# A recurrence with a feed-forward network beside it: plain fp32 products in four 32-column strips in place of split fp32r products

## The chip, the cores and the metric

The kernel runs on one core of one Trainium2 chip. The metric is the device time of one execution in microseconds, and the figure given is the median of several executions. TensorE is shown by the trace as two engines, PE (matmuls) and PEld (weight loads); DVE is VectorE, ACT is ScalarE, POOL is GpSimd, SP issues the DMAs. One plain fp32 matmul of the program stands in the trace as two records, an fp32r matmul as one.

## The reference, cut to what matters

Four layers act on x of shape (16, 256, 256), each added to its input. The first two (attention, a gated linear recurrence) are not touched but for a side job in the first. The third is a mixture of experts with a shared network, the fourth is a recurrence over 256 steps:

```python
# third layer: out is the sum over the routed experts
shared = jax.nn.gelu(context_c @ sw1 + sb1, approximate=True) @ sw2 + sb2
return out + shared
# fourth layer
xw = jnp.einsum('ntd,dh->nth', x, Wx) + b
def step(prev_h, xw_t):
    next_h = jnp.tanh(xw_t + prev_h @ Wh)
    return (next_h, next_h)
_, hs = jax.lax.scan(step, h0, jnp.swapaxes(xw, 0, 1))
```

sw1 is 256 x 1024, sw2 is 1024 x 256, Wx and Wh are 256 x 256.

## The kernel before, in words

All data lie transposed, features on the 128 partitions. The program has three blocks: attention and linear recurrence, then the experts, then the last stage, `shared_and_rnn`, which is the subject here.

An fp32 product is made in one of two ways. Plain: one matmul on fp32 operands. Split: each operand is parted into a high half rounded to fp32r and the rest (`xhi` and `xlo`, `ghi` and `glo`, weights in two versions), and three fp32r matmuls (high by high, high by rest, rest by high) add up in PSUM. The experts use the split form. Their weights are split once, by POOL in the attention block (`split_piece`, two instructions for each of 40 pieces of 128 x 512), written to DRAM and read again.

The last stage does two things at once. The recurrence has 256 steps. In step k TensorE multiplies the state by `wh` (`recur`, L1720: 2 halves of the contraction x 4 strips; the state is the stationary operand, 128 x 32, the weights move, 64 columns, and strip j writes PSUM partitions 32j to 32j+31), DVE transposes the result out of PSUM (L1825), ACT takes tanh (L1800), and its result is the state of step k+1. In even steps TensorE also computes x times `wx` for the next two steps (`drive`, L1731, the same shape). In odd steps DVE copies the bias into the PSUM bank used next (L1828).

Between the steps TensorE works off the shared network of the third layer for 14 chunks of 16 time steps (256 columns each; the first two chunks were done in the experts' block and are kept as `y0`). A generator, `all_ffn`, yields the matmuls in a fixed order and `quota(k)` says how many follow step k: 4 to 6 in the first 16 steps, then 5.75 on average, after 12 ahead of step 0. There are 96 matmuls a chunk: 8 up products and 8 down products of 2 x 3 fp32r matmuls, all with 128 x 128 weights and 256 columns. After an up product ACT takes gelu (L1809), then DVE splits the result (`split`: cast L1833, subtraction L1835), and down products read the split parts. When a chunk is done, DVE adds its two halves to x (`add_x`, L1846), which fills `xc`, the input of `drive` 16 steps later; it waits until POOL has used the buffer's former content (`staged_done`). POOL adds state and input for every chunk of 16 steps (L1873), and SP sends the sum out.

In-order engines: DVE serves the transposes, the splits and `add_x` from one queue, ACT tanh and gelu from one, TensorE everything from one.

Of the kernel before, what the change touches and what calls it, by code (L numbers as in the profile page):

```python
# [12 lines left out]
P = 128  # L13
# [97 lines left out]
def build(nc, x_tok, x_dm, small_in, mod_w, w_qkv, w_out, w_fih, ew1, ew2, sw1, sw2, wx, wh, out):  # L111
# [13 lines left out]
    with hold:  # L125
# [7 lines left out]
        halves = nc.dram_tensor("weight_halves", (NE + 1, 2, P, 2, DC * F), fp32).ap()  # L133
# [15 lines left out]
def attention(nc, env):  # L149
# [5 lines left out]
    with st:  # L155
# [68 lines left out]
        def piece(n):  # L224

            e, w, q = n // 8, n // 4 % 2, n % 4
            if w == 0:
                src = env["ew1"][e] if e < NE else env["sw1"]
                src = src[(q // 2) * P:(q // 2 + 1) * P, (q % 2) * PIECE:(q % 2 + 1) * PIECE]
            else:  # L230
                src = env["ew2"][e] if e < NE else env["sw2"]
                src = src[2 * q * P:2 * (q + 1) * P].rearrange("(c p) d -> p c d", p=P)
            return src, env["halves"][e, w, :, :, q * PIECE:(q + 1) * PIECE]
# [20 lines left out]
        def pieces_to(r):  # L254

            return max(0, 2 * (r + 1) + min(r + 1, 10))
# [1031 lines left out]
CH = 16  # L1288
NCH = T // CH
PIECE = 512  # L1290
PIECES = 8 * (NE + 1)
# [4 lines left out]
def experts(nc, env):  # L1296
# [9 lines left out]
    with st:  # L1306
        xhi = sb(st, "xhi", [P, DC, B, T], fp32r)
        xlo = sb(st, "xlo", [P, DC, B, T], fp32r)
        w1 = sb(st, "w1", [P, 2, 2, DC, F], fp32r)
        w2 = sb(st, "w2", [P, 2, 2, FC, D], fp32r)  # L1310
# [5 lines left out]
        y0 = raw1[:, :, 0:FIRST * T]  # L1316
# [15 lines left out]
        with ExitStack() as routed:  # L1332
            g = sb(routed, "g", [P, RING, T])
# [12 lines left out]
            room = env["wfih_sb"][:].rearrange("p c n -> p (c n)")  # L1346
# [24 lines left out]
            def _(sp):  # L1371
# [9 lines left out]
                load_weights(sp, JOBS, halves[NE:NE + 1], up_done, down_done)  # L1381
# [12 lines left out]
            def _(act):  # L1394
# [241 lines left out]
def shared_and_rnn(nc, env, ex):  # L1636
# [4 lines left out]
    xhi, xlo, w1, w2, wx, wh = (ex[k] for k in ("xhi", "xlo", "w1", "w2", "wx_sb", "wh_sb"))  # L1641
    N = B * CH
    BUF = TOP * B % 2
# [4 lines left out]
    ITEMS = 6  # L1648
    AHEAD = 12
    st = ExitStack()  # L1650
    with st:  # L1651
# [3 lines left out]
        staged = ex["raw1"][:, :, 2 * N:4 * N].rearrange("p s (t c b) -> p s t c b", t=CH, c=DC)  # L1655
        row1 = sb(st, "row1", [P, 2 * B])
        g = ex["raw2"][:, 0:RING]
        ghi = sb(st, "ghis", [P, RING, N], fp32r)
        glo = sb(st, "glos", [P, RING, N], fp32r)
# [8 lines left out]
        up_ok, gelu_ok, hi_ok, lo_ok, down_ok = (sem(st, n) for n in ("up_ok", "gelu_ok", "hi_ok", "lo_ok", "down_ok"))  # L1668
# [6 lines left out]

        FFN = 2 * ITEMS * FC

        def step_of(end):

            at = -1  # L1680
            taken = AHEAD
            while taken < end:
                at += 1
                taken += quota(at)
            return at
# [7 lines left out]
        def up_step(c, f):  # L1693
            return step_of(FFN * (c - FIRST) + (ITEMS * (f + 1) if f < 3 else 2 * ITEMS * f - ITEMS))

        def down_step(c):
            return step_of(FFN * (c + 1 - FIRST))

        gelus_in, splits_in, adds_in = ({k: [] for k in range(-1, T)} for _ in range(3))
        for c in range(FIRST, NCH):  # L1700
            for f in range(FC):
                k = up_step(c, f)
                gelus_in[k].append((c, f))
                splits_in[k + 1 if k >= 0 else k].append((c, f))
            k = down_step(c)
            adds_in[k + 1 if k >= 0 else k].append(c)
# [6 lines left out]
        def _(pe):  # L1713
# [20 lines left out]
            def ffn(c, xs):  # L1734

                for n in range(FC + 2):
                    if n < FC:
                        pe.wait_ge(gelu_ok, FC * (c - FIRST) + n + 1)
                        for k in range(DC):
                            whi, wlo = (w1[:, BUF, v, k, n * P:(n + 1) * P] for v in range(2))  # L1740
                            dst = ph[n % RING][:, 0:N]
# [5 lines left out]
                            if k == DC - 1:  # L1747
                                i.then_inc(up_ok, 1)
                            yield
                    if n >= 2:  # L1750
                        f = n - 2
                        pe.wait_ge(lo_ok, FC * (c - FIRST) + f + RING + 1)
                        if f == 0 and c > FIRST:
                            pe.wait_ge(x_ready, c)
                        hi, lo = ghi[:, f % RING], glo[:, f % RING]
                        for m in range(DC):
                            whi, wlo = (w2[:, BUF, v, f, m * P:(m + 1) * P] for v in range(2))
                            dst = py[:, m, 0:N]
                            nc.tensor.matmul(dst, whi, hi, start=(f == 0), stop=False)  # L1759
                            yield  # L1760
                            nc.tensor.matmul(dst, whi, lo, start=False, stop=False)  # L1761
                            yield
                            i = nc.tensor.matmul(dst, wlo, hi, start=False, stop=(f == FC - 1))  # L1763
# [4 lines left out]
            def all_ffn():  # L1768
                for c in range(FIRST, NCH):
                    yield from ffn(c, (slice(None), slice(0, B), slice(CH * c, CH * (c + 1))))  # L1770

            pe.wait_ge(ex["wxh_in"], 32)
            for w in range(2):
                for h in range(2):
                    pe.wait_ge(ex["w_in"][w][h][BUF], 16 * (TOP * B // 2 + 1))
            work = all_ffn()
            for _ in range(AHEAD):
                next(work, None)
            pe.wait_ge(row1_set, 1)
# [6 lines left out]
            for k in range(T):  # L1786
# [3 lines left out]
                for _ in range(quota(k)):  # L1790
                    next(work, None)

        @block.scalar
        def _(act):
            def recur(k):
                q, s, at = k // CH // 2, k // CH % 2, k % CH
                act.wait_ge(pre_ready, k + 1)
                if at == 0:
# [4 lines left out]
            for k in range(-1, T):  # L1803
                if k >= 0:
                    recur(k)
                for c, f in gelus_in[k]:
                    act.wait_ge(up_ok, FC * (c - FIRST) + f + 1)
                    act.wait_ge(lo_ok, FC * (c - FIRST) + f + 1)
                    nc.scalar.activation(g[:, f % RING], ph[f % RING][:, 0:N], ACT.Gelu_apprx_tanh,  # L1809
# [3 lines left out]
        def _(dve):  # L1813
            def bias_of_state():
                dve.wait_ge(zeroed, 2)
# [21 lines left out]
            def add_x(c):  # L1837
                s = c % 2
                if c >= FIRST:
                    dve.wait_ge(down_ok, FC * (c + 1 - FIRST) + RING)  # L1840
                dve.wait_ge(staged_done[s], 2 * PRIMED + 2 * (c // 2))
                for m in range(DC):
                    y = py[:, m, 0:N].rearrange("p (b t) -> p b t", b=B)
                    if c < FIRST:
                        y = ex["y0"][:, m].rearrange("p (b t) -> p b t", b=B)[:, :, CH * c:CH * (c + 1)]
                    i = nc.vector.tensor_tensor(xc[:, s, m].rearrange("p t b -> p b t"), XT[:, m, :, CH * c:CH * (c + 1)],  # L1846
                                                y, ALU.add)
                    i.then_inc(half_added if m == 0 else x_ready, 1)

            for k in range(-1, T):  # L1850
                if k >= 0:
                    recur(k)
                for c in adds_in[k]:
                    add_x(c)
                if k < 0:
                    for c in range(FIRST):
                        add_x(c)
                    bias_of_state()
                for c, f in splits_in[k]:
                    split(c, f)  # L1860

        @block.gpsimd
        def _(pool):
            nc.gpsimd.memset(row1[:], 0.0).then_inc(zeroed, 1)  # L1864
            pool.wait_ge(zeroed, 1)
            nc.gpsimd.memset(row1[0:1, :], 1.0).then_inc(row1_set, 1)
            nc.gpsimd.memset(hs[:], 0.0).then_inc(zeroed, 1)

            def stage(q, s):
                pool.wait_ge(h_ready, CH * (2 * q + s + 1) + 1)  # L1870
                pool.wait_ge(out_done[s], 16 * PRIMED + 16 * q)
# [3 lines left out]
            with pool.Fori(0, NCH // 2) as i:  # L1875
                stage(i, 0)
                stage(i, 1)
# [67 lines left out]
```

## Time and profile before

| | us |
|---|---|
| median of 3 executions | 1309.77 (1305.39 to 1312.52) |
| the profiled execution, its own time | 1305.88 |
| span of the profiled execution | 1304.1 |
| PE busy in the span | 1216.4 (93%) |
| DVE busy | 879.0 (67%) |
| ACT busy | 623.2 (48%) |
| POOL busy | 333.9 (26%) |

The span begins with the first and ends with the last instruction of the program; the profiled execution's own time is 1.8 us longer. The profile can split a span into stretches and give each engine's busy time in them, group instructions by line and shape, or list them in order of time. A matmul's record runs from when its first column enters to a modelled end, so records overlap: the distance from one start to the next tells what a matmul costs, not its length.

### The profile page before, as it was taken

How to read it: one execution, taken by the hardware profiler on the slowest of the kernel's cores; microseconds unless marked ns; L12 is line 12 of the kernel's file. 1: busy time of each engine (PE TensorE's matmuls, PEld its weight loads, DVE VectorE, ACT ScalarE, POOL GpSimd, SP SyncE). 2: the span in 40 equal slices, each digit the busy share in tenths (PEclk: the TensorE clock that was granted, in tenths of full speed). 3: DMA queues.
4: the chain of work that ended last, by engine and by line, in shares of the span. 5: the costliest groups of instructions: out<-in, count | busy, mean ns of one | idle time of the engine just before them, and what ended most of it. 6: DMA issues, size and time to landing. Idle time of an engine off the chain costs nothing. (4 is left out here: it accounts for less than half of the span.)

```text
span 1304.1 us, 34455 instructions
## 1 busy us (share of the span) xinstructions
PE 1216.4 (93%) x14104; PEld 961.0 (74%) x14104; DVE 879.0 (67%) x2047; ACT 623.2 (48%) x1168; POOL 333.9 (26%) x311
## 2 busy tenths in 40 slices
PE   3789999999999988499999999999999999999995
PEld 2456666766665433159999999999978888888883
DVE  6788888888775889957666666666655555555552
ACT  2377777777777879433333333333323333333331
POOL 1436566465552679600000000000010000000000
PEclk9699999999999999799999999999999999999995
DMA  9013242332212100059999999999900000000000
GB/s 359 3 50 99 85 136 74 123 99 86 87 50 82 64 1 1 0 203 397 378 368 360 368 363 371 365 366 361 370 11 19 11 19 11 20 11 19 11 19 18
DMA packets 82507, 190.39 MB, mean 146 GB/s; under 512 B 4144, under 2 KB 15536, under 8 KB 82096
## 3 DMA queue, kind: packets, MB, share of 16 engines
q1 hardware_dynamic: 82352, 188.21, 40.2%
q8 instruction: 112, 1.84, 0.6%
q14 instruction: 43, 0.35, 0.1%
HBM read 162.76 MB, written 25.17 MB: 144 GB/s over the span
## 5 line engine op out<-in xcount | busy, mean ns | idle before, releaser
L1417 ACT ACTIVATE g<-ph,b 128x256 f32<-128x256 f32 x256 | 121.6, 475 | 247.9 <-PE ph L1606 247.8
L693 DVE TENSOR_REDUCE mx<-pR 128x4 f32<-128x1024 f32 x128 | 156.4, 1225 | 62.7 <-PE pR L899 61.4
L1825 DVE STREAM_TRANSPOSE preT<-pr 128x64 f32<-128x64 f32 x256 | 63.9, 250 | 157.7 <-PE pr L1720 155.7
L1800 ACT ACTIVATE hs<-preT 128x32 f32<-128x32 f32 x256 | 58.8, 230 | 217.2 <-DVE preT L1825 217.0
L1526 DVE CAST ghi<-g 128x256 fp32r<-128x256 f32 x256 | 74.8, 292 | 128.2 <-ACT g L1417 128.0
L1622 PE MATMUL py<-ghi,w 128*128 128x256 f32 x512 | 145.7, 285 | 1.7 <-DVE glo L1528 1.6
L1604 PE MATMUL ph<-xhi,w 128*128 128x256 f32 x512 | 145.3, 284 | 0.0
L1605 PE MATMUL ph<-xlo,w 128*128 128x256 f32 x512 | 144.9, 283 | 0.0
L1623 PE MATMUL py<-glo,w 128*128 128x256 f32 x512 | 144.9, 283 | 0.0
L1624 PE MATMUL py<-ghi,w 128*128 128x256 f32 x512 | 144.9, 283 | 0.0
L1606 PE MATMUL ph<-xhi,w 128*128 128x256 f32 x512 | 144.9, 283 | 0.0
L490 ACT ACTIVATE raw<-pR 128x1024 f32<-128x1024 f32 x128 | 129.2, 1024 | 17.7 <-PE pR L908 16.1
L1720 PE MATMUL pr<-wh_sb,hs 128*32 128x64 f32 x4096 | 114.0, 231 | 10.2 <-ACT hs L1800 10.2
L1528 DVE TENSOR_TENSOR glo<-g,ghi 128x256 fp32r<-128x256 f32 x256 | 108.9, 426 | 8.8
L1720 PEld LDWEIGHTS pr<-wh_sb,hs 128*32 128x32 f32 x4096 | 71.4, 112 | 47.5 <-ACT hs L1800 15.5
L1873 POOL TENSOR_TENSOR raw<-xc,hs 128x256 f32<-128x256 f32 x32 | 23.5, 756 | 323.7 <-ACT hs L1800 323.7
L1864 POOL MEMSET row<- 128x32 f32 x1 | 0.1, 125 | 404.3 <-POOLq L1332 404.3
L1622 PEld LDWEIGHTS py<-ghi,w 128*128 128x128 f32 x512 | 98.2, 192 | 3.2 <-DVE glo L1528 3.1
L1605 PEld LDWEIGHTS ph<-xlo,w 128*128 128x128 f32 x512 | 98.3, 192 | 0.2 <-issue 0.2
L1604 PEld LDWEIGHTS ph<-xhi,w 128*128 128x128 f32 x512 | 98.3, 192 | 0.2 <-issue 0.2
L1606 PEld LDWEIGHTS ph<-xhi,w 128*128 128x128 f32 x512 | 98.3, 192 | 0.0
L1623 PEld LDWEIGHTS py<-glo,w 128*128 128x128 f32 x512 | 98.2, 192 | 0.0
(226 smaller groups left out, 2898.1 us busy)
## 6 DMA issues: line engine op xcount, KB each, us to landing
w<-weight_halves SPq DMA_DIRECT2D x132, 1024.0 KB, 8.0
weight_halves<-wparts SPq DMA_DIRECT2D x40, 512.0 KB, 3.9
modw<-in_ew SPq DMA_DIRECT2D x32, 256.0 KB, 4.5
xn<-in_x_tok SPq DMA_DIRECT2D x4, 1024.0 KB, 11.8
XT<-in_x_dm SPq DMA_DIRECT2D x2, 2048.0 KB, 14.6
out_dm<-raw SPq DMA_DIRECT2D x16, 256.0 KB, 2.0
modw<-in_sw SPq DMA_DIRECT2D x8, 256.0 KB, 4.5
raw<-in_sw SPq DMA_DIRECT2D x2, 1024.0 KB, 7.7
```

Of the source, the lines that this page charges most:

```text
L490: nc.scalar.activation(probs[:, j % 4], pR[k][:], ACT.Exp, scale=HD ** -0.5).then_inc(free[k], 1)
L693: nc.vector.reduce_max(mx[:, :, 2 * j:2 * j + 2].rearrange("p t s -> p s t"), pR[k][:].rearrange("p s (t k) -> p s t k", t=TC), AX.X).then ...
L1417: nc.scalar.activation(g[:, t % RING], ph[t % RING][:, 0:T], ACT.Gelu_apprx_tanh, bias=b1[:, n, f:f + 1]).then_inc(gelu_done, 1)
L1526: nc.vector.tensor_copy(ghi[:, t % RING], g[:, t % RING]).then_inc(hi_done, 1)
L1528: nc.vector.tensor_tensor(glo[:, t % RING], g[:, t % RING], ghi[:, t % RING].bitcast(fp32), ALU.subtract).then_inc(lo_done, 1)
L1604: nc.tensor.matmul(dst, whi, hi, start=(k == 0), stop=False)
L1605: nc.tensor.matmul(dst, whi, lo, start=False, stop=False)
L1606: i = nc.tensor.matmul(dst, wlo, hi, start=False, stop=(k == DC - 1))
L1622: nc.tensor.matmul(dst, whi, hi, start=(f == 0), stop=False)
L1623: nc.tensor.matmul(dst, whi, lo, start=False, stop=False)
L1624: i = nc.tensor.matmul(dst, wlo, hi, start=False, stop=(f == FC - 1))
L1720: i = nc.tensor.matmul(dst[QW * j:QW * (j + 1)], prev[:, c], quad(wh[:, c], j), start=False, stop=(c == DC - 1), skip_group_check=True)
```

## The change

The shared network of the last stage is computed in plain fp32. Its weights are taken from `raw1` and `raw2`, fp32 copies that are in SBUF since the end of the attention block; the split versions of the shared weights are no longer made (`PIECES` falls from 40 to 32), stored or read (`load_weights` of job `JOBS` is gone). Each product is issued as four matmuls with 128 x 32 weights (`strips`), the form that `recur` and `drive` have. Up products are made in two halves of 128 columns, an item each; down products stay at 256 columns. `quota(k)` now counts in halves: an up item counts 1 and a down item 2, 4 for each step, and 3 in every fourth step from step 64; nothing is issued ahead of step 0. The input x of the network is put together again by POOL as `xf = xhi + xlo` (`whole_x`, 128 x 512, one for each chunk). `split` is gone, gelu writes straight into `g` (4 buffers), and the down products read it. The two additions of `add_x` go into two successive steps. The memset of `hs` is cut in three, with `whole_x(2)` after the second; `y0` and `staged` have places of their own, and the copy into `y0` in the experts' block now waits for `b1_ready` first.

```diff
-PIECES = 8 * (NE + 1)
+PIECES = 8 * NE
...
-                load_weights(sp, JOBS, halves[NE:NE + 1], up_done, down_done)
...
                 act.wait_ge(down_first, FC)
+                act.wait_ge(b1_ready, 1)
                 nc.scalar.copy(y0, py[0][:, :, 0:FIRST * T]).then_inc(y_kept, 1)
-                act.wait_ge(b1_ready, 1)
...
         def quota(k):
 
-            if k < CH:
-                return (4, 6, 5, 6)[k % 4]
-            return (5 if k % 2 == 0 else 7) - (k % 8 in (2, 3))
+            return 3 if k >= 4 * CH and k % 4 == 2 else 4
...
+        def order():
+
+            for c in range(FIRST, NCH):
+                for n in range(FC + 2):
+                    if n < FC:
+                        for a in range(2 * DC):
+                            yield 1, (("up", c, n) if a == 2 * DC - 1 else None)
+                    if n >= 2:
+                        for m in range(DC):
+                            yield 2, (("down", c, n - 2) if m == DC - 1 else None)
...
+            def strips(dst, weights, moving, start, stop):
+
+                for j in range(QD):
+                    i = nc.tensor.matmul(dst[QW * j:QW * (j + 1)], weights[:, QW * j:QW * (j + 1)], moving, start=start, stop=stop)
+                return i
...
-                            nc.tensor.matmul(dst, whi, xhi[:, k][xs], start=(k == 0), stop=False)
-                            yield
-                            nc.tensor.matmul(dst, whi, xlo[:, k][xs], start=False, stop=False)
-                            yield
-                            i = nc.tensor.matmul(dst, wlo, xhi[:, k][xs], start=False, stop=(k == DC - 1))
...
+                        for a in (0, HALF):
+                            for k in range(DC):
+                                moving = xf[:, c % 2, k].rearrange("p b t -> p (b t)")[:, a:a + HALF]
+                                i = strips(ph[n % RING][:, a:a + HALF], raw1[:, k, n * P:(n + 1) * P], moving, k == 0, k == DC - 1)
...
-            def split(c, f):
-                dve.wait_ge(gelu_ok, FC * (c - FIRST) + f + RING + 1)
-                dve.wait_ge(down_ok, FC * (c - FIRST) + f + 1)
-                nc.vector.tensor_copy(ghi[:, f % RING], g[:, f % RING]).then_inc(hi_ok, 1)
-                dve.wait_ge(hi_ok, FC * (c - FIRST) + f + 1)
-                nc.vector.tensor_tensor(glo[:, f % RING], g[:, f % RING], ghi[:, f % RING].bitcast(fp32), ALU.subtract).then_inc(lo_ok, 1)
...
+            def whole_x(c):
+                if c >= FIRST + 2:
+                    pool.wait_ge(up_ok, FC * (c - 1 - FIRST))
+                at = slice(CH * c, CH * (c + 1))
+                nc.gpsimd.tensor_tensor(xf[:, c % 2], xhi[:, :, :, at].bitcast(fp32), xlo[:, :, :, at].bitcast(fp32), ALU.add).then_inc(xf_ready, 1)
```

On TensorE, an odd and an even step of the recurrence early in the last stage. `pr` is the recurrence's PSUM, `phs` that of the up products, `pys` that of the down products. Before:

```order
L1720 MATMUL pr1<-wh_sb,hs 32x64 [waits h_ready]
L1720 MATMUL pr1<-wh_sb,hs 32x64 x7
L1742 MATMUL phs0<-xhi,w1 128x256
L1744 MATMUL phs0<-xlo,w1 128x256
L1746 MATMUL phs0<-xhi,w1 128x256
L1759 MATMUL pys<-ghis,w2 128x256 [waits lo_ok]
L1761 MATMUL pys<-glos,w2 128x256
L1763 MATMUL pys<-ghis,w2 128x256
L1720 MATMUL pr0<-wh_sb,hs 32x64 [waits h_ready]
L1720 MATMUL pr0<-wh_sb,hs 32x64 x7
L1731 MATMUL pr1<-wx_sb,xc 32x64 [waits bias_set,x_ready]
L1731 MATMUL pr1<-wx_sb,xc 32x64 x7
```

And of the changed kernel, the end of step 2 and step 3 (a matmul here writes 32 partitions, so 16 of them make two halves of an up product over both halves of the contraction, and 8 make a whole down product):

```order
L1727 MATMUL pr0<-wx_sb,xc 32x64 [waits bias_set,x_ready]
L1727 MATMUL pr0<-wx_sb,xc 32x64 x7
L1733 MATMUL phs2<-xf,raw 32x128 [waits gelu_ok]
L1733 MATMUL phs2<-xf,raw 32x128 x15
L1716 MATMUL pr1<-wh_sb,hs 32x64 [waits h_ready]
L1716 MATMUL pr1<-wh_sb,hs 32x64 x7
L1733 MATMUL pys<-gs,raw 32x256 [waits gelu_ok]
L1733 MATMUL pys<-gs,raw 32x256 x7
```

Every matmul of the changed stage is 32 wide in its output partitions; before, 5 to 7 matmuls of 128 partitions stood between two recurrence groups.

On DVE, at step 16, where chunk 2 of the shared network is added to x. Before:

```order
L1825 STREAM_TRANSPOSE preT<-pr 128x64 [waits step_done]
L1846 TENSOR_TENSOR xc<-XT,pys 128x16x16 [waits staged_done0,down_ok]
L1846 TENSOR_TENSOR xc<-XT,pys 128x16x16
L1825 STREAM_TRANSPOSE preT<-pr 128x64 [waits step_done]
L1828 COPY pr<-bias_tile 128x64 [waits pre_ready]
L1825 STREAM_TRANSPOSE preT<-pr 128x64 [waits step_done]
L1833 CAST ghis<-raw 128x256 [waits down_ok,gelu_ok]
L1835 TENSOR_TENSOR glos<-raw,ghis 128x256 [waits hi_ok]
```

Of the changed kernel:

```order
L1813 STREAM_TRANSPOSE preT<-pr 128x64 [waits step_done]
L1827 TENSOR_TENSOR xc<-XT,pys 128x16x16 [waits staged_done0,down_ok]
L1813 STREAM_TRANSPOSE preT<-pr 128x64 [waits step_done]
L1816 COPY pr<-bias_tile 128x64 [waits pre_ready]
L1827 TENSOR_TENSOR xc<-XT,pys 128x16x16
```

The second addition has moved behind the next step's transpose and bias copy, and the cast and subtraction are no longer on the engine; the wait for `staged_done0` still stands before the first addition, ahead of step 17's transpose.

## Rows read from the trace of the kernel before

**Rows 1.** Window, whole stage: us; busy and instructions by engine; granted TensorE clock; DMA.

```profile
960.00:1270.00 310.00, 309.98 (x6793) 257.32 (x6782) 165.81 (x588) 101.83 (x338) 20.69 (x28) 1.00 0.04 15
```

**Rows 2.** Windows, recurrence matmuls of L1720 alone, 16 records a step; granted clock.

```profile
1041.98:1237.71 195.73, 62.02 (x2304) 38.76 (x2304) 1.00 0.04 15
1272.70:1279.30 6.60, 2.81 (x96) 1.76 (x96) 0.89 0.02 4
1280.60:1298.60 18.00, 9.15 (x224) 5.78 (x224) 0.50 0.05 17
```

**Rows 3.** Timeline of TensorE, steps 4 and 5: start, length, engine, line, operation.

```profile
960.98 0.43 PE L1720 MATMUL pr<-wh_sb,hs 128*32 128x64 f32 x16
...
961.23 0.41 PE L1731 MATMUL pr<-wx_sb,xc 128*32 128x64 f32 x16
...
961.57 0.39 PE L1759 MATMUL pys<-ghis,w 128*128 128x256 f32 x1
...
961.79 0.28 PE L1761 MATMUL pys<-glos,w 128*128 128x256 f32 x1
...
961.91 0.28 PE L1763 MATMUL pys<-ghis,w 128*128 128x256 f32 x1
...
962.02 0.28 PE L1742 MATMUL phs<-xhi,w 128*128 128x256 f32 x1
...
962.24 0.43 PE L1720 MATMUL pr<-wh_sb,hs 128*32 128x64 f32 x16
...
962.60 0.39 PE L1744 MATMUL phs<-xlo,w 128*128 128x256 f32 x1
```

**Rows 4.** Timeline of one step after the shared network has ended.

```profile
1274.91 0.43 PE L1720 MATMUL pr<-wh_sb,hs 128*32 128x64 f32 x16 [0.63 <-ACT hs L1800]
...
1275.41 0.25 DVE L1825 STREAM_TRANSPOSE preT<-pr 128x64 f32<-128x64 f32 x1 [0.55 <-PE pr L1720]
1275.69 0.23 ACT L1800 ACTIVATE hs<-preT 128x32 f32<-128x32 f32 x1 [0.84 <-DVE preT L1825]
...
1275.97 0.43 PE L1720 MATMUL pr<-wh_sb,hs 128*32 128x64 f32 x16 [0.41 <-ACT hs L1800]
```

**Rows 5.** Timeline: last matmul of the shared network, last recurrence matmul.

```profile
1272.08 0.39 PE L1763 MATMUL pys<-ghis,w 128*128 128x256 f32 x1
...
1298.69 0.65 PE L1720 MATMUL pr<-wh_sb,hs 128*32 128x64 f32 x16 [0.63 <-ACT hs L1800]
```

**Rows 6.** Timeline in the attention block: one call of values, L925.

```profile
218.79 1.07 PE L925 MATMUL pO<-raw,vp 128*32 128x256 f32 x16
```

**Rows 7.** Groups by line, attention stretch 200:480: busy us, mean ns.

```profile
L925 PE MATMUL pO<-raw,vp 128*32 128x256 f32 x672 | 45.0, 385 | 0.3 <-ACT oraw L476 0.3
...
L925 PEld LDWEIGHTS pO<-raw,vp 128*32 128x32 f32 x672 | 17.6, 109 | 15.6 <-issue 3.5
```

**Rows 8.** Groups by line and shape, last stage: busy us, mean ns, idle.

```profile
L1809 ACT ACTIVATE raw<-phs,small 128x256 f32<-128x256 f32 x112 | 52.5, 472 | 24.4 <-PE phs L1746 20.5 <-DVE glos L1835 0.7
```

**Rows 9.** Timeline at the start of the last stage.

```profile
952.36 1.81 POOL L1867 MEMSET hs<- 128x2048 f32 x1
...
954.65 0.23 DVE L1818 COPY bias_tile<-pr 128x64 f32<-128x64 f32 x1 [0.27 <-PE pr L1783]
...
955.50 0.43 PE L1720 MATMUL pr<-wh_sb,hs 128*32 128x64 f32 x16
```

**Rows 10.** Timeline around step 16, TensorE left out.

```profile
976.48 1.43 POOL L1873 TENSOR_TENSOR raw<-xc,hs 128x256 f32<-128x256 f32 x2 [22.32 <-ACT hs L1800]
...
978.01 1.07 DVE L1846 TENSOR_TENSOR xc<-XT,pys 128x256 f32<-128x256 f32 x2 [0.71 <-POOL raw L1873]
```

**Rows 11.** Groups by line, GpSimd, whole span.

```profile
L252 POOL TENSOR_TENSOR wparts<-modw,wparts 128x512 fp32r<-128x512 f32 x40 | 51.2, 1280 | 3.2
...
L250 POOL CAST wparts<-modw 128x512 fp32r<-128x512 f32 x40 | 25.2, 629 | 89.5 <-DMA modw<-in_ew 81.9 <-DMA modw<-in_sw 7.6
```

**Rows 12.** Timeline at the start of the expert products.

```profile
578.55 1.01 ACT L1410 COPY raw<-py 128x1024 f32<-128x1024 f32 x1 [2.69 <-PE py L1570]
```

More of the change, by code:

```diff
@@ L132, in build @@
         pieces_out = [sem(hold, f"pieces_out{q}") for q in range(2)]
-        halves = nc.dram_tensor("weight_halves", (NE + 1, 2, P, 2, DC * F), fp32).ap()
+        halves = nc.dram_tensor("weight_halves", (NE, 2, P, 2, DC * F), fp32).ap()
         def vec(name, a=None, z=None):
@@ L1674, in quad @@
             return w.rearrange("p (k q) -> p k q", q=P)[:, :, QW * j:QW * (j + 1)]
[L1676 to L1685, printed above, removed]
-        def quota(k):
-            if k < CH:
-                return (4, 6, 5, 6)[k % 4]
-            return (5 if k % 2 == 0 else 7) - (k % 8 in (2, 3))
[L1693 to L1699, printed above, removed]
+        def quota(k):
+            return 3 if k >= 4 * CH and k % 4 == 2 else 4
[8 more added lines that the diff above has]
+                            yield 2, (("down", c, n - 2) if m == DC - 1 else None)
+        counts, ended, left, item = [0] * T, {}, 0, order()
+        for k in range(T):
+            left += quota(k)
+            while left > 0:
+                size, what = next(item, (left, None))
+                left -= size
+                counts[k] += 1
+                ended[what] = k
+        gelus_in, adds_in = ({k: [] for k in range(T)} for _ in range(2))
         for c in range(FIRST, NCH):
             for f in range(FC):
[L1702 to L1706, printed above, removed]
+                gelus_in[ended["up", c, f]].append((c, f))
+            for m in range(DC):
+                adds_in[ended["down", c, FC - 1] + 1 + m].append((c, m))
         def half(k):
@@ L1769, in all_ffn @@
                 for c in range(FIRST, NCH):
-                    yield from ffn(c, (slice(None), slice(0, B), slice(CH * c, CH * (c + 1))))
+                    yield from ffn(c)
             pe.wait_ge(ex["wxh_in"], 32)
-            for w in range(2):
-                for h in range(2):
-                    pe.wait_ge(ex["w_in"][w][h][BUF], 16 * (TOP * B // 2 + 1))
             work = all_ffn()
-            for _ in range(AHEAD):
-                next(work, None)
-            pe.wait_ge(row1_set, 1)
+            pe.wait_ge(row1_set, 2)
             for half_pair in steps:
@@ L1789, in _ @@
                     drive(k // 2 + 1)
-                for _ in range(quota(k)):
+                for _ in range(counts[k]):
                     next(work, None)
@@ L1850, in _, with add_x @@
[L1850 to L1860, printed above, removed]
+            def add_x(c, m):
+                s = c % 2
+                if m == 0:
+                    if c >= FIRST:
+                        dve.wait_ge(down_ok, FC * (c + 1 - FIRST) + KEEP)
+                    dve.wait_ge(staged_done[s], 2 * PRIMED + 2 * (c // 2))
+                y = py[:, m, 0:N].rearrange("p (b t) -> p b t", b=B)
+                if c < FIRST:
+                    y = ex["y0"][:, m].rearrange("p (b t) -> p b t", b=B)[:, :, CH * c:CH * (c + 1)]
+                nc.vector.tensor_tensor(xc[:, s, m].rearrange("p t b -> p b t"), XT[:, m, :, CH * c:CH * (c + 1)],
+                                        y, ALU.add).then_inc(half_added if m == 0 else x_ready, 1)
@@ L1862, in _ @@
+            for m in range(DC):
+                add_x(0, m)
+            bias_of_state()
+            for k in range(T):
+                recur(k)
+                if k in (1, 3):
+                    add_x(1, k // 2)
+                for c, m in adds_in[k]:
+                    add_x(c, m)
         @block.gpsimd
         def _(pool):
-            nc.gpsimd.memset(row1[:], 0.0).then_inc(zeroed, 1)
-            pool.wait_ge(zeroed, 1)
+            nc.gpsimd.memset(row1[:], 0.0).then_inc(row1_set, 1)
@@ L1866, in _ @@
+            nc.gpsimd.memset(hs[:, 1, CH - 1], 0.0).then_inc(zeroed, 1)
+            pool.wait_ge(row1_set, 1)
             nc.gpsimd.memset(row1[0:1, :], 1.0).then_inc(row1_set, 1)
[L1867 to L1871, printed above, removed]
+            nc.gpsimd.memset(hs[:, 0], 0.0).then_inc(zeroed, 1)
+            def whole_x(c):
[3 more added lines that the diff above has]
+                nc.gpsimd.tensor_tensor(xf[:, c % 2], xhi[:, :, :, at].bitcast(fp32), xlo[:, :, :, at].bitcast(fp32), ALU.add).then_inc(xf_ready, 1)
@@ L1872, in stage @@
+            def stage(c):
+                s = c % 2
+                pool.wait_ge(h_ready, CH * (c + 1) + 1)
+                pool.wait_ge(out_done[s], 16 * PRIMED + 16 * (c // 2))
                 for e in range(2):
@@ L1874, in stage @@
                                             hs[:, s, e::2, :, half(e + 1)], ALU.add).then_inc(staged_done[s], 1)
-            with pool.Fori(0, NCH // 2) as i:
-                stage(i, 0)
-                stage(i, 1)
+            whole_x(FIRST)
+            nc.gpsimd.memset(hs[:, 1, 0:CH - 1], 0.0).then_inc(zeroed, 1)
+            whole_x(FIRST + 1)
+            for c in range(NCH):
+                stage(c)
+                if c + FIRST + 2 < NCH:
+                    whole_x(c + FIRST + 2)
         @block.sync
```

81 lines of the change are left out of this document (30 added, 51 removed).

## The prediction

> **What bounds the kernel now.** Only the last stage changes much, so I cut it out first with the view of stretches. From 960 to 1270 us TensorE is busy for 309.98 of 310 us at the full granted clock [rows 1]; DVE is busy for 166 and ACT for 102 us. TensorE looks like the bound, but busy time counts a matmul's record to its modelled end, so the next question is what a step costs and what is in it. The recurrence's matmuls alone give the rate: 2304 records are 144 steps in 195.73 us, 1.359 us a step [rows 2].
>
> The timeline of two steps shows the parts [rows 3]. Step 4 starts at 960.98, its `recur` takes 0.25 us until `drive` starts, `drive` 0.34 until the first matmul of the shared network, that one 0.22 until the second; the next two spacings are 0.12 and 0.11; the last one is followed by `recur` of step 5 after 0.22. Step 5 has no `drive`, and its first network matmul starts 0.36 after `recur`. So a network matmul costs 0.12 in a row of its like, but wherever 32-wide matmuls and 128-wide ones meet, more passes: 0.36 against 0.25 on leaving `recur`, 0.22 against 0.12 after the first wide one, 0.22 against 0.12 before `recur`. That is 0.31 us a step that moves no column.
>
> How far could a step shrink? After the network has ended, at the same clock, `recur` starts 1.06 us apart (1274.91 to 1275.97): 0.50 until DVE's transpose starts, 0.28 until tanh starts, 0.28 until the next `recur` [rows 4]. This chain is the floor, and the stage stands 0.30 a step above it. TensorE's own queue sets the step today, the chain is next.
>
> **The change, part by part.** *Price of a strip product.* The last stage of before has no strip matmul with 128 or 256 moving columns, but the attention block has one: a call of L925 is 8 matmuls of 128 x 32 weights and 256 columns, 16 records in four passes over the four strips. Together they last 1.07 us [rows 6] with a mean record of 385 ns [rows 7], so three pass distances are at most 0.69, at most 0.23 each; `recur` gives the same from below, four passes of 64 columns in 0.25 [rows 3], 0.06 a pass. Two passes make a whole fp32 product with 128 x 128 weights: 0.46 at the most for 256 columns, and about 0.43 if the start-up of the first pass and the stagger of the strips are taken off. I take 0.44 for a down item and 0.22 for an up item (half as many columns). The same product in three fp32r matmuls costs 0.36. A chunk has 8 x 4 up items and 8 x 2 down items, 64 units of 0.22, and 14 chunks 896 units, 197 us; before it was 1344 x 0.12 = 161 us. By itself the arithmetic loses 36 us.
>
> *What it gives back.* All matmuls of the stage are now 32 wide, so the 0.31 a step goes, over 234 steps 73 us. This is the step on which all rests. The Trainium skill, TensorEngine Tiling (Array Packing), Key Properties, says that changing the tiling mode drains the engine; the trace agrees, with the 0.36 for 0.25 above. I keep 0.24 for `recur` and 0.22 for `drive`.
>
> *Steps.* Steps 0 to 63 carry 4 units each: even 0.24 + 0.22 + 0.88 = 1.34, odd 1.12, both above the chain's 1.06. From step 64 on it is 3.75 units on average, 0.24 + 0.11 + 0.825 = 1.175; but down items can't be halved, so some steps get 5 units and some 2, and the light ones end at 1.06. Worked through in order, with each step the longer of its own TensorE work and 1.064, steps 64 to 234 come to 205.5 us, 1.20 each. Steps 1 to 63 take 77.5 with the stalls below, step 0 takes 1.4. Network work ends with step 234. Then 20 steps of the chain alone: before, the granted clock was still 0.89 on average up to 7 us after the network's end [rows 2, 5], and 0.50 behind that, where 14 steps took 18.00 us, 1.287 each [rows 2]. I take 7 steps at 1.064 and 13 at 1.287, 24.2 us. From first to last `recur` that is 1.4 + 77.5 + 205.5 + 24.2 = 308.6 us; before, 955.50 to 1298.69 [rows 5, 9], 343.2.
>
> *Start.* Before, DVE's copy of the state waited for the end of the 1.81 us memset at 954.17, then `bias_tile` followed at 954.65 and `recur` at 955.50 [rows 9]; 12 network matmuls stood ahead of it on TensorE. Now a 64-element memset is enough, and DVE is held by two `add_x` instead of four, 0.5 us each. I put `recur` at 954.3, 1.2 us earlier. Its first network item waits for `xf`, behind a memset of 1024 elements (0.9, half of 1.81) and one 128 x 512 addition on POOL: 1.28 by the nearest row [rows 11]. That is 954.85, and step 0 takes 1.4 instead of 1.34.
>
> *DVE and ACT.* The 112 casts and 112 subtractions leave DVE, which was busy for 166 of 310 us [rows 1] and is no bound, so this is worth nothing directly. At step 16 the addition waited for POOL's two sums of 1.43 us and started at 978.01, 1.46 after its step's `recur`, with 1.07 us for both halves [rows 10]. Now only one half (0.53) stands before the next transpose: it ends 2.0 after `recur` of step 16, the transpose was due at 1.34 + 0.50 = 1.84, and 0.11 us remains once TensorE's slack is used. The same at steps 32, 48 and 64, 0.45 us together. Gelu, 472 ns [rows 8], waits for an up product that ends about 0.23 after the next `recur` starts, and so is done at 0.70; tanh is due at 0.78 [rows 4]. It is hidden by 0.08 us; if it came later, each lost tenth would count in half of the steps.
>
> *POOL, pieces, `y0`.* `whole_x` runs once per 16 steps, two chunks ahead of its use. Eight pieces fewer free POOL of 8 x 1.28 us of subtractions [rows 11] and their casts in the attention block. If all of it were on the path it would give some 15 us, but POOL itself stood idle there for 90 us ahead of the casts, waiting for the pieces to arrive [rows 11], so I take 0. The copy into `y0` was released by TensorE's last product [rows 12], and the gelu behind it in the same queue needs `b1` anyway, so the new order of waits costs nothing; were `b1` late, it would be the copy's 1.0 us once.
>
> *Sum.* 343.2 - 308.6 + 1.2 = 35.8 us. Span 1304.1 becomes 1268.3, the profiled execution 1270; its time of 1305.88 lies 3.9 below the median of the runs shown. Against the median, 1309.8 - 36 = 1273.8; with the first steps' and pieces' small change I say 1273.
>
> **The rivals.**
> *The chain is longer than it looks (0.12).* With gelu and tanh or POOL and DVE in each other's way a step takes not 1.064 but 1.20 at least. For it: only 0.08 us of cover for gelu. Against: in the timeline of before, the 0.50 from `recur` to transpose and the 0.28 to tanh without gelu [rows 4] held in most steps with it. The same walk with 1.20 gives 13.8 us more, 1287.
> *Half of the gap stays (0.03).* If part of the 0.31 belongs to the wait for `h_ready` and not to the width, 0.155 a step costs 32 us: 1306, within a measurement's reach of no change.
> *All of it stays (0.05), slower.* If the gap comes with every change of operands or of PSUM bank, the new stage has it too: 0.31 a step, and the walk ends 32.7 us later than today, 1342. It decides from 0.17 us a step on. Against: consecutive wide matmuls change from up to down product at 0.11 to 0.12, and `recur` to `drive` costs nothing extra [rows 3].
> *Weight loads don't overlap (0.03), slower.* Each pass would wait for its own 109 ns load [rows 7]: a unit costs 2 x (0.11 + 0.11) = 0.44, a down item 0.66, and the walk gives 108 us over today, 1417. Against: the call of 1.07 us holds four passes of 256 columns and has no room for three more loads [rows 6]. The Trainium skill, TensorE: Matmul & The Clock Gate, Part 3, says that a load overlaps running matmuls only when its row group differs, and all strips here share their rows; the trace contradicts it for strips beside each other.
> The rest (0.01) is the granted clock of 0.50 in this stage, at which a unit costs twice as much; while TensorE was busy the clock was 1.00 [rows 1].
>
> **How the numbers follow.** The main case has 0.76. Its own range goes from passes at the lower bound (64 columns in 0.06, less the start-up: 0.213 a unit, `recur` 0.224: 9 us less) to the upper one (0.23 and 0.25: 10 us more), 1264 to 1283. The range of 8 in 10 takes in the longer chain: 1262 to 1289. A measurement of this kernel can tell about 0.5% from no change. Faster by more than that: main case and long chain, 0.88; the same 0.03 (half of the gap); slower 0.09.
>
> **What would show it.** In the changed trace: recurrence matmuls 16 steps apart by 19.2 us from step 64 on instead of 21.7; four strips of 128 columns 0.22 apart; `recur` to the first network matmul 0.24 in odd steps; gelu ending before tanh is due; `recur` of step 0 near 954.3 and the last one near 1263. I am wrong if a gap of 0.1 or more stays before or behind `recur`, if odd steps are above 1.15, or if the granted clock falls before the network ends.

## The result, and the profile after

The changed kernel takes 1311.72 us (median of 20 runs, 1306.21 to 1318.08), the kernel before 1309.7 us (20 runs, 1304.06 to 1312.68). The ratio is 1.0025, with an interval of 1.0013 to 1.0037: 0.25% slower, where 1273 and a range of 1262 to 1289 had been forecast. The span of the profiled execution is 1309.3 us (before 1304.1) at a mean granted clock of 0.973.

First the same stretch as in [rows 1], a little shorter, in both kernels. Windows of the kernel before; after length, busy time and instructions of PE, PEld, DVE, ACT and POOL come the granted clock, the DMA share and GB/s:

```profile
970.00:1230.00 260.00, 259.98 (x5701) 215.79 (x5703) 139.44 (x493) 85.34 (x283) 17.85 (x24) 1.00 0.04 15
```

The same window of the changed kernel:

```profile
970.00:1230.00 260.00, 241.43 (x8886) 200.61 (x8879) 79.43 (x306) 83.84 (x279) 32.14 (x36) 1.00 0.05 17
```

The first column after the window is its length in us; each engine's count of records stands in brackets. DVE has lost 60 us, as meant. TensorE has 56% more matmul records, and it now stands idle for 18.6 us, which it didn't before. The recurrence's matmuls alone give what a step costs, as in [rows 2]. Windows of the changed kernel, L1716, steps 64 to 223:

```profile
1045.19:1263.59 218.40, 80.41 (x2561) 62.80 (x2561) 1.00 0.05 17
```

That is 1.365 us a step, against 1.359 before and 1.20 forecast. But most single steps are as short as forecast. Timeline of TensorE, changed kernel, a step without `drive` that carries five units (an up item is one unit, a down item two):

```profile
1151.25 0.43 PE L1716 MATMUL pr<-wh_sb,hs 128*32 128x64 f32 x16
1151.47 0.87 PE L1733 MATMUL phs<-xf,raw 128*32 128x128 f32 x24
1152.13 0.64 PE L1733 MATMUL pys<-gs,raw 128*32 128x256 f32 x8
1152.56 0.33 PE L1716 MATMUL pr<-wh_sb,hs 128*32 128x64 f32 x9
```

`recur` to network 0.22, three up items 0.66, one down item 0.43: the forecast's 0.24, 0.22 a unit and 0.44. The loss stands elsewhere. Timeline of the changed kernel around a long step:

```profile
1098.68 0.43 PE L1716 MATMUL pr<-wh_sb,hs 128*32 128x64 f32 x16
...
1099.80 0.41 PE L1716 MATMUL pr<-wh_sb,hs 128*32 128x64 f32 x16
...
1100.24 0.61 PE L1733 MATMUL pys<-gs,raw 128*32 128x256 f32 x8
...
1100.56 0.23 ACT L1789 ACTIVATE hs<-preT 128x32 f32<-128x32 f32 x1 [0.46 <-DVE preT L1813]
1101.57 0.38 PEld L1733 LDWEIGHTS phs<-xf,raw 128*32 128x32 f32 x16 [1.19 <-issue]
1101.57 0.65 PE L1733 MATMUL phs<-xf,raw 128*32 128x128 f32 x16 [0.71 <-issue]
...
1102.03 0.41 PE L1716 MATMUL pr<-wh_sb,hs 128*32 128x64 f32 x16
```

The step at 1098.68 lasts 1.12 us, exactly the sum. The next lasts 2.23 instead of 1.34: after a down item, due to end its 0.44 at 1100.68, the next load and matmul start together at 1101.57, 0.89 us late. The profile names no engine and no semaphore that they wait for ("issue"); the state for the next `recur` was ready at 1100.79 and `recur` started at 1102.03, behind them in the queue. The groups by line put the idle time down to the same cause (page of the changed kernel; mean ns, then idle time):

```profile
L1733 PE MATMUL phs<-xf,raw 128*32 128x128 f32 x3584 | 144.0, 275 | 10.5 <-issue 10.4
...
L1716 PE MATMUL pr<-wh_sb,hs 128*32 128x64 f32 x4096 | 130.7, 228 | 15.0 <-ACT hs L1789 9.2 <-issue 4.8
```

Such pauses come about 127 matmul records apart, or a multiple of that (254, 381, 509). That number has a counterpart in the queues. DMA view, changed kernel, 970:1230 (packets, MB, share):

```profile
q1 hardware_dynamic: 1728, 3.15, 3.2%
q8 instruction: 70, 1.15, 1.9%
```

The same queue and window before:

```profile
q8 instruction: 45, 0.74, 1.2%
```

The queue that brings instructions moved 70 packets of 16 KB in 260 us, one per 3.71 us and per 127 matmul records (with their loads). Before it was 45 packets, one per 5.8 us, and also 127 records each.

The packets' own times in the trace tie the pauses to them. The one that began at 1098.90 had landed at 1100.23; the long pause above ended at 1101.57, 1.34 us later, and the next packet began at 1102.62, 1.05 us after that. Between 970 and 1230 us TensorE has 33 places where a matmul starts more than 0.45 us after the one before it: every one ends 1.25 to 1.61 us after a packet has landed. A packet takes 1.12 us on average, and no two overlap.

The stage needs 4096 + 2048 + 3584 + 1792 = 11520 records, 90.7 packets, 336 us at 3.71; the forecast gave it 308.6 and it took 348.2.

### The profile page after: what moved, and what is told of

Same layout as the page of the kernel before. It is cut to its first block and busy times, and to the rows that moved or that the text cites. A ratio compares the mean times of both kernels' runs of the same rounds, so it can differ in the third digit from the quotient of the medians.

```text
span 1309.3 us, 42133 instructions
## 1 busy us (share of the span) xinstructions
PE 1198.6 (92%) x18136; PEld 946.4 (72%) x18136; DVE 805.0 (61%) x1823; ACT 622.5 (48%) x1168; POOL 335.7 (26%) x311
## 5 line engine op out<-in xcount | busy, mean ns | idle before, releaser
L1733 PE MATMUL phs<-xf,raw 128*32 128x128 f32 x3584 | 144.0, 275 | 10.5 <-issue 10.4
L1716 PE MATMUL pr<-wh_sb,hs 128*32 128x64 f32 x4096 | 130.7, 228 | 15.0 <-ACT hs L1789 9.2
L1733 PE MATMUL pys<-gs,raw 128*32 128x256 f32 x1792 | 136.8, 380 | 2.4 <-issue 1.3
L1716 PEld LDWEIGHTS pr<-wh_sb,hs 128*32 128x32 f32 x4096 | 99.8, 113 | 48.2 <-ACT hs L1789 34.2
L1733 PEld LDWEIGHTS phs<-xf,raw 128*32 128x32 f32 x3584 | 106.9, 111 | 19.4 <-issue 17.2
L1603 PEld LDWEIGHTS ph<-xhi,w 128*128 128x128 f32 x512 | 98.3, 192 | 0.2 <-issue 0.2
```

What stands on the lines that cost most here:

```text
L1603: nc.tensor.matmul(dst, whi, hi, start=(k == 0), stop=False)
L1716: i = nc.tensor.matmul(dst[QW * j:QW * (j + 1)], prev[:, c], quad(wh[:, c], j), start=False, stop=(c == DC - 1), skip_group_check=True)
L1733: i = nc.tensor.matmul(dst[QW * j:QW * (j + 1)], weights[:, QW * j:QW * (j + 1)], moving, start=start, stop=stop)
```

## The experiments

**Theory A, supply.** TensorE's instructions can't arrive faster than about one packet per 3.7 us (29 ns a matmul record) for long; the 128-column halves doubled the instructions of the up products and pushed the stage over this. **Theory B.** POOL's `whole_x`, or the strips' reads of `xf`, disturb TensorE or its supply. **A third reading.** The pauses belong to TensorE's own pace with many short passes.

**Up products whole.** Against the changed kernel; same arithmetic, 9728 records instead of 11520:

```diff
-                        for a in range(2 * DC):
-                            yield 1, (("up", c, n) if a == 2 * DC - 1 else None)
+                        for a in range(DC):
+                            yield 2, (("up", c, n) if a == DC - 1 else None)
...
-                        for a in (0, HALF):
-                            for k in range(DC):
+                        for k in range(DC):
+                            moving = xf[:, c % 2, k].rearrange("p b t -> p (b t)")
+                            i = strips(ph[n % RING][:, 0:N], raw1[:, k, n * P:(n + 1) * P], moving, k == 0, k == DC - 1)
```

> The changed kernel with up products whole (one strip group of 256 columns in place of two of 128; an item counts 2). The same columns and the same strips, but 1792 fewer matmul records in the last stage (9728 instead of 11520). Theory A (the instruction stream feeds TensorE no faster than 128 matmul records with their loads, one 16 KB block, in about 3.73 us, so the stage of the changed kernel is 90 blocks long): 76 blocks need 3.1 to 3.9 us of TensorE work each, most stalls go, the walk through the steps gives 303 us from first to last recur instead of 348, span about 1266 to 1272. Theory B (POOL's additions of xf, or SBUF reads by strips, hold TensorE up): the time stays at 1309 within 5 us.

1265.92 us (1265.11 to 1266.4), ratio to before 0.9678 [0.9645, 0.9712]. One loop taken out of the change makes the kernel 3.2% faster than the one at which the change started. The stage was expected at 303 us and took 304.5. Timeline and windows of TensorE in this kernel:

```profile
1201.53 0.43 PE L1716 MATMUL pr<-wh_sb,hs 128*32 128x64 f32 x16
1201.78 1.05 PE L1733 MATMUL phs<-xf,raw 128*32 128x256 f32 x16
1202.64 0.41 PE L1716 MATMUL pr<-wh_sb,hs 128*32 128x64 f32 x16
1202.86 0.41 PE L1727 MATMUL pr<-wx_sb,xc 128*32 128x64 f32 x16
1203.09 1.05 PE L1733 MATMUL pys<-gs,raw 128*32 128x256 f32 x16
1203.95 0.41 PE L1716 MATMUL pr<-wh_sb,hs 128*32 128x64 f32 x16
```

```profile
970.00:1230.00 260.00, 259.92 (x8620) 180.77 (x8613) 92.50 (x354) 97.75 (x323) 35.04 (x40) 1.00 0.06 19
```

Steps of 1.11 (1.087 at the median) without `drive` and 1.31 with it, and next to no idle time (0.08 us). The instruction queue in the same window:

```profile
q8 instruction: 68, 1.11, 1.8%
```

That is a packet per 3.82 us, just under the limit.

**Up products in quarters.** The changed kernel with `for a in (0, HALF // 2, HALF, HALF + HALF // 2)`, 64 columns each and two products between two yields, so the columns between two steps stay the same; 15104 records.

> The changed kernel with up products in quarters of 64 columns: the same columns, 3584 more matmul records in the last stage (15104, 118 blocks). Theory A: 118 blocks x 3.73 = 440 to 447 us for the stage instead of 348, span about 1405. Theory B: no change beyond 10 us, since a pass of 64 columns costs 0.056 us and one of 128 columns 0.109.

1413.57 us, ratio 1.0808 [1.0759, 1.0857]; the stage took 452.1 us, 5 more than the upper end of what was expected. The window and the instruction queue again, then a stretch of the timeline:

```profile
970.00:1230.00 260.00, 187.32 (x8928) 159.05 (x8925) 61.40 (x234) 64.29 (x213) 24.01 (x27) 1.00 0.04 14
```

```profile
q8 instruction: 70, 1.15, 1.9%
```

```profile
1101.21 1.08 PE L1733 MATMUL phs<-xf,raw 128*32 128x64 f32 x64
1102.11 0.41 PE L1716 MATMUL pr<-wh_sb,hs 128*32 128x64 f32 x16
1102.33 0.29 PE L1727 MATMUL pr<-wx_sb,xc 128*32 128x64 f32 x7
1103.38 0.35 PE L1727 MATMUL pr<-wx_sb,xc 128*32 128x64 f32 x9 [0.76 <-issue]
```

TensorE is now idle for 73 us of 260, yet the records of the window hardly differ from those of the changed kernel, 8928 against 8886, and the packets are 70 again. Its pauses over 0.45 us, 64 of them, all end 1.21 to 1.54 us after a packet has landed. This is the ceiling. And the third reading falls by the first row: 64 records went out in 0.90 us, 14 ns each, twice as fast as the mean of the window. TensorE can take short passes at that pace. The pause stands in the middle of the next `drive`, between two records of the same form.

**Half of the columns left out.** The changed kernel; from the second chunk on each up half moves 64 of its 128 columns, so half of the up products' columns aren't computed; the instructions stay.

> The changed kernel (up products in two halves) in which, from the second chunk on, each half moves only 64 of its 128 columns, so a quarter of the shared network's hidden columns is not computed anew (left out). The number of matmuls is the same, 11520 records in the stage; their columns are fewer: 416 units fall from 0.22 to 0.11 us, 46 us of TensorE work. Theory A (instruction stream, 90 blocks of 128 records at 3.73 us): the stage stays at 340 to 348 us, the time at 1305 to 1312. If the stalls of the changed kernel had their cause in what the matmuls do (columns, SBUF reads, PSUM writes), the time would fall by 30 us or more, to 1280 or lower.

1312.43 us, ratio 1.002 [0.9999, 1.0042]; first to last `recur` 351.15 us against 348.22, 3 above what Theory A expected. Groups of this kernel:

```profile
L1733 PE MATMUL phs<-xf,raw 128*32 128x64 f32 x3328 | 86.3, 221 | 19.9 <-issue 19.9
```

Nearly a quarter of the network's column time is gone (busy in the window 213.49 instead of 241.43) and nothing is won: each column saved became a wait for instructions. The time follows the number of records and not the work in them.

**Without `whole_x`.** The changed kernel without POOL's sums; the up products read `xhi` as fp32, so the low part of x is left out.

```diff
-                                moving = xf[:, c % 2, k].rearrange("p b t -> p (b t)")[:, a:a + HALF]
+                                moving = xhi[:, k, a // CH:(a + HALF) // CH, CH * c:CH * (c + 1)].bitcast(fp32)
...
-            whole_x(FIRST)
...
-            whole_x(FIRST + 1)
```

> The changed kernel without POOL's 14 additions whole_x: the up products read xhi alone, in place, so the shared network leaves out the low part of x. Theory A: the same number of instructions on TensorE, so the same time within 3 us (the first network item no longer waits for POOL, which may give 1 us). Theory B: the stalls shrink and the time falls by 10 us or more.

1310.59 us, ratio 1.0016 [0.9996, 1.0035]; POOL's busy time in the window went from 32.14 to 17.12 us, the packets stayed at 70. So POOL's sums aren't the cause. The up products still read fp32 here; that half of Theory B falls by two other runs: half as many columns read changed nothing, and whole up products read all of them with next to no idle time.

**Full width.** Whole up products as in the first experiment, and one matmul with 128 x 128 weights in place of the four strips (7040 records). This is the undoing of the strips alone:

```diff
-                for j in range(QD):
-                    i = nc.tensor.matmul(dst[QW * j:QW * (j + 1)], weights[:, QW * j:QW * (j + 1)], moving, start=start, stop=stop)
-                return i
+                return nc.tensor.matmul(dst, weights, moving, start=start, stop=stop)
```

> As e1_whole_up, but each product of the shared network is one plain fp32 matmul with 128 x 128 weights instead of four strips. 7040 records in the stage, so the instruction stream is no limit under either theory. The gaps between widths should come back: 0.31 us a step over 234 steps, 73 us, of which about 5 us hide behind the chain. Stage about 365 to 371 us from first to last recur, span 1330 to 1336. If the gaps had nothing to do with the width of the matmuls, it would be as fast as e1_whole_up, 1266 to 1272.

1339.43 us, ratio 1.0236 [1.0199, 1.0273]. Timeline of TensorE:

```profile
1103.69 0.43 PE L1716 MATMUL pr<-wh_sb,hs 128*32 128x64 f32 x16
1104.05 1.13 PE L1732 MATMUL pys<-gs,raw 128*128 128x256 f32 x4
1105.11 0.43 PE L1716 MATMUL pr<-wh_sb,hs 128*32 128x64 f32 x16
1105.36 0.41 PE L1727 MATMUL pr<-wx_sb,xc 128*32 128x64 f32 x16
1105.69 1.13 PE L1732 MATMUL phs<-xf,raw 128*128 128x256 f32 x4
```

0.36 us from `recur` to the network is back, as in [rows 3]. The steps are 1.42 and 1.645 instead of 1.087 and 1.31: 0.335 a step for nothing but the width, since a pass inside a product costs 0.215 us in both kernels. The stage takes 376.8 us, 72 more than with strips and 6 more than was expected. So the strips do what the forecast rested on, which had put 0.31 a step and 73 in all.

**Two strips of 64.** As the first experiment, with `for j in range(2)` and 64 columns of weights in each: half of its network records, 7936 in the stage (the expectation's 8384 is miscounted). It asks whether the gap belongs to the full width or to any change of width.

> e1_whole_up with the shared network's products in two strips of 64 columns instead of four of 32; 8384 records, so no limit by the instruction stream. If the gap between widths comes with any change of strip width (32 to 64 and back), it is back as in e3_full_width, 0.33 us a step: 1339. If only the change between strips and the full width costs, it is as fast as e1_whole_up, 1266.

1327.14 us, ratio 1.0145 [1.0115, 1.0175]; the steps cost 1.375 and 1.598, 0.288 more than with strips of 32, and the time is 12 us under the expectation for a gap at any change. Timeline:

```profile
1100.40 0.43 PE L1716 MATMUL pr<-wh_sb,hs 128*32 128x64 f32 x16
1100.76 1.08 PE L1733 MATMUL phs<-xf,raw 128*64 128x256 f32 x8
1101.78 0.43 PE L1716 MATMUL pr<-wh_sb,hs 128*32 128x64 f32 x16
```

Again 0.36 behind `recur`. The change between 32 and 64 costs nearly as much as that between 32 and 128, so the half-way layout saves instructions but keeps most of the gap.

**Additions together.** The first experiment with `adds_in[ended["down", c, FC - 1] + 1]` for both halves.

> e1_whole_up with both additions of add_x in one step again. Each takes about 0.55 us on DVE behind the transpose; two end up to 0.3 us after the next transpose is due, at 14 chunk ends, of which TensorE's slack hides part: 1 to 3 us more, 1267 to 1269. If DVE has enough slack, no difference.

1269.28 us, ratio 0.9703 [0.9673, 0.9732], an interval that overlaps the first experiment's. In the traces the stage is 2.6 us longer (307.12 against 304.53), of which 0.45 is two more steps of the tail at the lower clock; the waits stand where a chunk ends. Timeline at step 17, where DVE's two additions in one hold the transpose:

```profile
995.30 1.43 POOL L1858 TENSOR_TENSOR staged<-xc,hs 128x256 f32<-128x256 f32 x2 [17.16 <-ACT hs L1788]
...
996.83 1.05 DVE L1826 TENSOR_TENSOR xc<-XT,pys 128x256 f32<-128x256 f32 x2 [0.79 <-POOL staged L1858]
...
997.74 0.22 DVE L1812 STREAM_TRANSPOSE preT<-pr 128x64 f32<-128x64 f32 x1
...
998.27 0.43 PE L1716 MATMUL pr<-wh_sb,hs 128*32 128x64 f32 x16 [0.36 <-ACT hs L1788]
```

**A warm tail.** The first experiment, and after the network's end one strip product with no use behind each `recur` and `drive`:

```diff
+                if k > ended["down", NCH - 1, FC - 1]:
+                    strips(ph[k % RING][:, 0:N], raw2[:, 0, 0:P], raw1[:, 0, 0:N], True, True)
```

> e1_whole_up with one dummy product (four strips, 256 columns, result not used) behind each recurrence step after the shared network has ended. In e1 the last 14 steps ran at the lower clock, 1.287 us each instead of 1.064. If the granted clock stays at 1.00 with TensorE about 60% busy, 14 x 0.22 = 3.1 us less, about 1262.8. If it falls all the same, the dummies lengthen each step (0.86 us of strips at half clock before the next recur): 1266 or a little more.

1262.73 us (1262.01 to 1263.79), ratio 0.9651 [0.9623, 0.968], the lowest median of this study, 46 us under the 1308.88 of the kernel before beside it. The interval overlaps the first experiment's, so the gain is read from the traces. Windows of the tail, first without these products (first experiment), then with them:

```profile
1241.70:1258.40 16.70, 11.06 (x304) 7.94 (x304) 4.40 (x19) 2.94 (x14) 0.00 (x0) 0.50 0.06 19
```

```profile
1236.00:1255.00 19.00, 16.98 (x564) 8.51 (x556) 6.32 (x26) 4.12 (x18) 1.42 (x2) 1.00 0.05 18
```

With the granted clock at 1.00 (2.4 GHz) instead of 0.50 (1.2 GHz) each step of the tail takes 1.065 us instead of 1.287, and the stage 301.4 instead of 304.5.

**Warm at the start too.** Four more such products ahead of step 0.

> e6_warm_tail with four more dummy products (strips, 256 columns, results not used) ahead of step 0, two before and two behind the bias rows, where TensorE stands idle for about 2 us and the clock is at 0.50 afterwards: step 0 took 2.56 us in e1_whole_up instead of 1.4. If they keep the clock up, step 0 is about 1 us shorter and the time about 1261.7; if the products run at the lower clock themselves (0.86 us each), they delay drive and recur of step 0 and the time is 1263 to 1265.

1263.16 us (1260.67 to 1266.8), ratio 0.9658 [0.9615, 0.97]. Step 0 went from 2.56 to 1.31 us in the trace, but the stage took 301.9 us against 301.4 with the warm tail alone, and in the medians the two can't be told apart. Steps 1 to 63 lost more than that again, 77.9 us against 76.2. Step 2 lasts 1.59 instead of 1.31: `recur` of step 3 starts at 957.86, 1.31 us after a packet has landed at 956.55, so at least this loss is one more pause of supply. The expectation named two outcomes; the time is that of the second, without its condition, since the added products ran at full pace.

## Why the prediction was wrong

The step that failed is *Steps*, in the words "each step the longer of its own TensorE work and 1.064". There is a third limit, the supply of instructions, and it decides here. From step 64 on a step carries 24 records of `recur` and `drive` on average and 3.75 units of 6 records, 46.5 together; at 127 records per 3.71 us that is 1.358 us, and 1.365 was measured. The forecast priced the columns of a product and never its instructions; it put that term at nothing. Its 1.20 would have asked for 38.7 records a us. The changed kernel was given 34.2, the one with quarters 34.3, and whole up products need 33.2.

From first to last `recur` the stage falls into three parts, by the starts of steps 0, 64, 224 and 255. The forecast's 205.5 us for 171 steps is shared out by number:

| steps | forecast | up products whole | changed kernel |
|---|---|---|---|
| 0 to 63 | 78.9 | 79.1 | 89.8 |
| 64 to 223 | 192.3 | 188.3 | 218.4 |
| 224 to 255 | 37.4 | 37.2 | 40.0 |
| all | 308.6 | 304.5 | 348.2 |

The second column shows that the sum was right within 4 us for a kernel that stays under this limit, and the third what the limit takes: 44 us. The visible idle time is smaller (18.6 us in 260), since a record's modelled end lies some 0.2 us behind the moment at which the next one is due, and the start of each pause lies under it.

Point by point:

- *Price of a strip product*: right. 0.22 a unit, 0.44 a down item; measured 0.22 and 0.43, 0.215 a unit where up products are whole.
- *What it gives back*: right, 0.335 a step instead of 0.31. That changing the tiling mode drains the engine (the Trainium skill, TensorEngine Tiling (Array Packing), Key Properties) fits these traces also between strips of 32 and of 64, where the change in and out costs 0.288 us.
- *The rivals*. A longer chain: no; steps of 1.087 with gelu in them rule out 1.20. Half or all of the gap stays: no, 0.22 behind `recur`. Weight loads that don't overlap: no; up halves went 0.11 a pass, the length of their own load, with no gap. None of the rivals was what happened, though its time lay between two of them.
- *Start*: right but for step 0. `recur` came 1.9 us after POOL's first memset of the stage, forecast 2.2, before 3.4. That it stands at 955.40 and not at 954.3 is the earlier part of the program, 1.4 us later in this execution. But TensorE had stood idle for 1.76 us ahead of the bias rows, and at a granted clock of 0.54 over steps 0 and most of 1, step 0 took 2.56 us and step 1 1.47: 1.5 us over the forecast. Before, 12 network matmuls stood there and step 0 took 1.55. Timeline and window of the changed kernel:

```profile
953.49 0.12 POOL L1842 MEMSET row<- 128x32 f32 x1 [404.59 <-POOLq L1331]
...
953.93 0.43 PE L1770 MATMUL pr<-small,row 128*32 128x64 f32 x16 [1.76 <-POOL row L1845]
...
955.40 0.72 PE L1716 MATMUL pr<-wh_sb,hs 128*32 128x64 f32 x16
```

```profile
955.40:959.00 3.60, 3.60 (x110) 3.60 (x104) 0.50 (x2) 0.70 (x2) 2.54 (x3) 0.54 0.02 5
```

- *DVE and ACT*: with whole up products steps 1 to 63 took 76.5 us where the forecast had 77.5 with the additions' stalls in it, and spreading them is worth some 2 us in the traces. *POOL*: nothing, as said; the stage's first memset came no earlier, at 953.49 against 952.12.
- The tail's 20 steps behind the network had four at full clock, not seven: 24.8 us instead of 24.2.

The account of the spans: 1.4 later start, 1.5 less ahead of `recur`, 5.0 more in the stage, 0.3 behind it, together the 5.2 us between 1304.1 and 1309.3.

What the forecast could have seen: cut into windows of 20 us, the trace before has none with more than 461 matmul records, 23 a us ([rows 1] have 22). The forecast asked for 38.7 and never compared the two, though where the limit lies can't be read from that trace. The call of L925 [rows 6], from which it took the price of a pass, has 16 records in 1.07 us, but such a burst, like the 64 records in 0.90 us with quarters, says nothing of 300 us.

Of the 3.7 us a packet only 1.12 is transfer. The order of times (a packet lands, TensorE goes on 1.25 to 1.61 us later, the next packet begins 1.0 to 1.9 us after that, 1.14 at the median) reads like a round trip with one packet under way at a time, and not like a queue that is full: 1.15 MB moved on it in the window, 1.9% of the DMA engines' time. No run varies that order, so this reading is argued and not shown. Whether the instruction streams of the other engines take from it stays open too.

## What to carry to other kernels

Count instructions per microsecond as well as columns: a product in four fp32 strips is eight matmul records with eight loads where full width has two and two, so strips want a moving operand as wide as can be had (256 columns here, where 128 were over the limit), and the count times the 29 ns measured here has to stay under the stage's time. Where idle time of TensorE is put down to "issue" at regular distances in records, look at the instruction queue in the DMA view before any semaphore. While TensorE waits on the last chain of a kernel, products without use can keep it at full clock, as they did here in two kernels, if they end before the chain needs the engine.

## What was not expected of the hardware

- A packet of the instruction queue holds 127 matmul records with their loads (126.0 to 127.5 in the eleven kernels). In dense stretches one comes per 3.71 us: 70, 70, 70 and 69 packets in 260 us in the changed kernel, with quarters, without `whole_x` and with half of the columns.
- After a packet has landed, 1.2 to 1.6 us pass until a TensorE that stands still goes on: all 97 pauses over 0.45 us in the windows of the changed kernel and of quarters.
- Ahead of that limit TensorE takes far more, 64 records of 64 columns in 0.90 us.
- The change from 32-wide to 64-wide strips and back costs 0.288 us a step, hardly less than that to full width, 0.335.
- One strip product a step kept the granted clock at 1.00 where the recurrence alone fell to 0.50.
